# Windowed attention and gated network over 192 tiles: softmax in the score banks, small value products on two row groups, network input in its own bank, new orders

## The reference

```
for i in range(6):
    x = attn_layer(shift_tokens(x), Wqkv[i], q_scale[i], k_scale[i], Wo[i]) + x
    x = ffn_layer(shift_tokens(x), ln_g[i], ln_b[i], W1[i], b1[i], W2[i], b2[i]) + x

attn_layer:
    q, k, v = split(x @ Wqkv)                  # 16 heads of 64
    q = l2norm(q) * q_scale;  k = l2norm(k) * k_scale
    q, k = rotary(q), rotary(k)                # q*cos*scale + rotate_half(q)*sin*scale
    sim  = q @ k of the own and the previous window of 32 rows, masked
    out  = softmax(sim) @ v;   return out @ Wo
ffn_layer:
    xn = (x - mean) / sqrt(var + 1e-5) * g + b
    a, gate = split(xn @ W1 + b1);  return a * gelu(gate) @ W2 + b2
```

## Time and profile before

| what | value |
|---|---|
| median of 3 runs (lowest to highest) | 3764.9 us (3754.34 to 3772.09) |
| the profiled execution | 3773.0 us |
| its span, first to last instruction | 3771.0 us |
| mean granted TensorE clock | 0.962 |
| busy: PE, DVE, ACT, POOL | 3375.2, 3287.8, 2435.9, 2810.7 us |

### The profile page before, as it was taken

How to read it: one execution, slowest core, us unless ns; L and a number is a source line. 1 busy time by engine, 2 the same in 40 slices (tenths; PEclk the granted TensorE clock), 3 DMA queues, 4 the chain that set the end, 5 groups by cost and what they waited for, 6 DMA issues and landing times.

```text
span 3771.0 us, 107872 instructions
## 1 busy us (share of the span) xinstructions
PE 3375.2 (90%) x45916; PEld 2204.0 (58%) x46108; DVE 3287.8 (87%) x2914; ACT 2435.9 (65%) x3945; POOL 2810.7 (75%) x1265
## 2 busy tenths in 40 slices
PE   5758999998999999999998999899999999999987
PEld 3325665665665665665666666565666656666664
DVE  6758999998999988999898998898988988998992
ACT  4645766766766766666666676666666666666764
POOL 4457788778787778778777778877777887887771
PEclk9879999999999999999999999999999999999996
DMA  2001111121111111111111111121111111111111
GB/s 72 1 1 36 36 34 38 34 58 41 35 34 39 34 51 44 39 34 35 36 52 44 33 35 35 31 50 44 39 33 34 38 46 45 39 37 35 34 37 36
DMA packets 129694, 141.98 MB, mean 38 GB/s; under 512 B 35388, under 2 KB 73152, under 8 KB 129216
## 3 DMA queue, kind: packets, MB, share of 16 engines
q1 hardware_dynamic: 129216, 135.09, 14.5%
HBM read 19.62 MB, written 2.10 MB: 6 GB/s over the span
## 4 chain that ended last, share of the span: by engine, by line
PE 33%; DVE 23%; POOL 18%; issue 12%; ACT 4%; SPq 3%; DMA 2%; POOLq 0%; ACTq 0%; DVEq 0%
PE bank L570 10%; POOL rr L1138 8%; POOL swp L1148 5%; PE mid L620 4%; DVE Pr L1362 4%; DVE rot L1398 4%; PE mid L579 4%; DVE raw L1390 4%; PE bank L639 4%; PE bank L668 3%; DVE rot L1404 3%; PE mid L607 2%; PE mid L627 2%; DVE ss L1384 2%; PE bank L676 2%
## 5 line engine op out<-in xcount | busy, mean ns | idle before, releaser
L1148 POOL TENSOR_TENSOR swp<-raw,TS 128x1024 f32<-128x1024 f32 x384 | 899.6, 2370 | 622.0 <-DVE raw L1390 622.0
L570 PE MATMUL bank<-wqkv,xs 128*128 128x512 f32 x2304 | 1206.9, 627 | 24.1 <-DMA xs<-F 8.6
L1138 POOL TENSOR_TENSOR rr<-ssm,nhalf 128x32 f32<-128x32 f32 x192 | 1214.8, 6327 | 16.0
L896 ACT ACTIVATE raw<-bank 128x512 f32<-128x512 f32 x768 | 434.6, 592 | 545.0 <-DVE rot L1404 483.8
L579 PEld LDWEIGHTS mid<-ident,rot 128*128 128x128 f32 x3072 | 367.8, 143 | 387.7 <-issue 335.9
L579 PE MATMUL mid<-ident,rot 128*128 128x128 f32 x3072 | 444.6, 278 | 132.7 <-DVE rot L1404 127.3
L1384 DVE TENSOR_REDUCE ss<-sq 128x16 f32<-128x1024 f32 x384 | 463.6, 1207 | 112.1 <-ACT sq L904 111.3
L570 PEld LDWEIGHTS bank<-wqkv,xs 128*128 128x128 f32 x2304 | 387.3, 193 | 289.9 <-issue 194.0
L1390 DVE TENSOR_TENSOR raw<-raw,rr 128x2048 f32<-128x2048 f32 x192 | 469.3, 2444 | 42.6 <-POOL rr L1138 42.6
L1398 DVE TENSOR_TENSOR rot<-raw,TC 128x2048 f32<-128x2048 f32 x192 | 442.2, 2303 | 52.6 <-PE mid L579 51.1
L1404 DVE TENSOR_TENSOR rot<-rot,swp 128x2048 f32<-128x2048 f32 x192 | 440.2, 2292 | 21.0 <-DVE rot L1398 1.4
(11 more groups left out here) (132 smaller groups left out, 4340.8 us busy)
## 6 DMA issues: line engine op xcount, KB each, us to landing
PT<-PTd SPq DMA_DIRECT2D x1344, 64.0 KB
xs<-F SPq DMA_DIRECT2D x192, 64.0 KB, 1.9
BT<-PTd SPq DMA_DIRECT2D x192, 64.0 KB
wqkv<-d_wqkv SPq DMA_DIRECT2D x36, 256.0 KB, 2.8
fwo<-d_fwo SPq DMA_DIRECT2D x6, 512.0 KB, 4.3
d_out<-X SPq DMA_DIRECT2D x8, 256.0 KB, 2.3
w<-d_w SPq DMA_DIRECT2D x6, 341.0 KB
w<-d_w SPq DMA_DIRECT2D x6, 128.0 KB
```

The costliest lines, as they stand in the source:

```text
L570: nc.tensor.matmul(bank[bk][:, :], xs[:, j, :], wqkv[:, c, :], start=True, stop=True)\
L1138: pool.tensor_tensor(rr[:, :], ssm[:, :], nhalf[:, :], ALU.pow).then_inc(rr_ready, 1)
L1148: last = pool.tensor_tensor(dst[:, :, :, t, :], src[:, :, :, 1 - t, :], tab.unsqueeze(2).broadcast_to([P, 2, HEADS, 32]), ALU.mult)
```

## The change

1. `less_max` writes its result back into banks 3 and 4 instead of `Pr`; `exps`, `sums` and the input of `probs` are in the banks too. PE's `scores` of the next tile therefore waits for `probs` (`prob_ready`) and no longer for `less_max` (`sub_ready`).
2. `BT` is filled in two parts (heads of u < 4 on partitions 96 to 127, of u >= 4 on partitions 64 to 95), and a new tile `VT` holds the previous tile's last V rows for u >= 4 on partitions 64 to 95. The small products alternate between the two row groups and between banks 2 and 5. A tile of j > 0 has 10 DMAs instead of 8, one of j = 0 has 7.
3. `centred` is written to bank 7, which the network's other products use, instead of bank 6; `out_proj` of a batch's first tile waits for `attn_to_sbuf` and no longer for `ffn_normed`.
4. New orders on all engines. `qk_back` 2 and 3 move one slot earlier. ACT's first copy of a tile waits for `cos_part` and `sin_part` of the tile two before and no longer for `rotated`.

More of the change, by code:

```diff
@@ L417, in loads_and_moves @@
                 next_ffn(l)
-                for q in range(5):
+                for q in range(6):
                     for i in range(TPB):
@@ L439, in _ @@
                 fetch(DEPTH, m)
-            for m in range(-5, 0):
+            for m in range(-4, 0):
                 move(DEPTH, m)
@@ L693, in slot @@
                     step(c, 2, qk_back, 0, True)
[L694 to L697, removed]
+                    after(c, (3, qkT_out[1]), (5, oT_out), (3, qkT_out[3]))
+                    step(c, 2, qk_back, 3, False)
+                    after(c, (0, raw_out[0]), (4, v_out[0]), (1, raw_out[3]))
@@ L698, in slot @@
+                    step(c, 0, proj, 3, False, 1)
+                    after_batch(c, (3, yo_ready), (3, lin_out[2]), (3, ge_ready[2]), (3, ge_ready[1]), (3, ge_ready[0]), (3, lin_out[0]), (3, lin_out[1]), (3, nT_out), (3, xn_ready))
+                    batch(c, 2, centred)
                     after(c, (2, qkT_out[0]), (3, qkT_out[2]), (5, oT_out))
-                    after(c, (3, qkT_out[3]), (3, qkT_out[1]), (5, oT_out))
+                    after(c, (2, qkT_out[3]), (3, qkT_out[1]), (5, oT_out))
@@ L722, in slot @@
-                    batch(c, 2, ffn_in, 0, 1, False, 7)
-                    after(c, (4, sub_ready))
-                    step(c, 3, scores)
+                    after(c, (4, prob_ready))
+                    step(c, 3, scores)
+                    after(c, (4, v_out[0]), (1, raw_out[3]), (1, raw_out[0]))
+                    step(c, 0, proj, 0, False, 1)
+                    after_batch(c, (2, xn_ready), (3, yo_ready), (3, lin_out[2]), (3, ge_ready[2]), (3, ge_ready[1]), (3, ge_ready[0]), (3, lin_out[0]), (3, lin_out[1]), (3, nT_out))
@@ L804, in slot @@
+                    step(c, 2, qk_back, 2, False)
                     step(c, 4, out_proj)
@@ L1006, in slot @@
                     step(c, 4, o_to_sbuf)
                     step(c, 0, squares, 1)
+                    step(c, 3, to_v, 4)
+                    step(c, 2, qk_to_sbuf, 2)
+                    step(c, 3, to_v, 5)
                     step(c, 2, qk_to_sbuf, 1)
-                    step(c, 3, to_v, 4)
+                    batch(c, 2, ffn_normed)
                     batch(c, 2, ffn_affine)
-                    step(c, 3, to_v, 5)
-                    step(c, 2, qk_to_sbuf, 2)
-                    step(c, 2, qk_to_sbuf, 3)
@@ new lines, in slot @@
+                    step(c, 3, exps)
+                    batch(c, 2, lin_to_sbuf, 0)
+                    step(c, 0, to_raw, 3, False)
+                    step(c, 4, o_to_sbuf)
+                    step(c, 0, squares, 1)
+                    step(c, 3, to_v, 4)
+                    step(c, 2, qk_to_sbuf, 2)
+                    batch(c, 2, gelu, 0)
+                    batch(c, 2, gelu, 1)
+                    step(c, 3, to_v, 5)
+                    batch(c, 2, gelu, 2)
+                    step(c, 2, qk_to_sbuf, 1)
+                elif c % TPB == 2:
+                    step(c, 0, to_raw, 1, True)
@@ L1424, in slot @@
                     step(c, 3, sums)
+                    batch(c, 2, ffn_stats)
                     step(c, 3, sums_inverse)
+                    step(c, 3, probs)
                     step(c, 0, sumsq, 1)
-                    step(c, 3, probs)
                     step(c, 3, probs_back)
@@ L1466, in slot @@
                     step(c, 1, rotated)
-                    batch(c, 1, ffn_stats)
                     step(c, 2, maxes)
@@ L1470, in slot @@
                     step(c, 0, normed)
-            slots(4, slot)
+            slots(8, slot)
             for b in range(B - 2, B):
```

269 lines of the change are left out of this document (124 added, 145 removed).

## The result

| what | value |
|---|---|
| median of the changed kernel's runs (lowest to highest) | 3612.2 us (3608.0 to 3612.9) |
| median of the kernel before, same chip | 3761.3 us (3754.3 to 3772.1) |
| ratio, with its 95% interval | 0.961 (0.958 to 0.964) |
| the profiled execution, its span | 3608.0 us, 3606.2 us |
| mean granted TensorE clock | 0.980 |

The change makes the kernel 149 us faster, 4%. The forecast was 3645 us, range 3500 to 3775.

What follows compares the result with a forecast made beforehand. DVE and PE, filled nearly alike, were taken as the bound. DVE work 62.8, gaps 1.0 and waits 5.4 make 69.2 us per batch against 71.7; 2.5 x 48 = 120 off 3765 gives 3645 us, range 3500 to 3775.

Steps and rivals of the forecast that it cites:

- Part 1: Softmax in the banks: `probs` falls from 1.88 to 1.22 us, `less_max` and `exps` stay at 1.22 and 1.05.
- the doubling rival: In-place bank operations cost double: DVE gets 4.9 us more per batch, 74.1, or 3880 us; chance 0.03.
- The new wait for `probs`: PE's `scores` waits for `probs`: nothing in slots 1 to 3, at worst 1 us per batch in slot 0.
- 2.4 per batch on DVE (65.2 becomes 62.8): DVE's busy time per batch in us, with some 0.6 us off `probs` in each of 4 tiles.
- the sum: DVE's batch: work 62.8, gaps 1.0, waits 5.4, together 69.2 us against 71.7 before.
- Part 2: Small products on two row groups: 0.55 us instead of 1.05, 1.5 us off PE per batch.
- fits below: PE's work of 64.6 us per batch stays under DVE's 69.2.
- the 1 to 2 named: `pv` on PE stands 1 to 2 us for band DMAs in slots 1 and 3.
- Part 3: Network in bank 7 and `rstd` early: the stall of `ffn_normed` for `rstd` goes, 1.9 us off the mean batch.
- long batch: A batch of 75.4 us where an ordinary one takes 70.0, with `ffn_normed` waiting 3.9 us for `rstd`.
- Part 4: New waits of the order, from ACT's copies and gelus in slots 1 and 2: 5.4 us of DVE waits per batch.
- The slower rival: ACT's chain in slots 1 and 2 stalls PE 4.5 us and lowers the clock every batch: 3851 us; chance 0.12.

Runs made afterwards that it cites:

- a_no_small: The changed kernel with the small products back on one row group and 8 band DMAs per tile: 3620.9 us, ratio 0.965.
- b_wait: The kernel before with one wait more, DVE's `normed` waits for `rstd` in slot 3: 3770.4 us, ratio 1.003.
- the orders alone: The changed kernel with softmax back in SBUF and small products on one row group, keeping new orders and the network's bank: 3743.7 us, ratio 0.999.
- a_act: The changed kernel with two swaps on ACT, `to_v` 5 ahead of gelu 1 and `qk_to_sbuf` 1 ahead of gelu 2: 3491.3 us, ratio 0.931.
- part 1 alone in the old order, b_banks: The kernel before with only the softmax in the banks, orders and small products as before: 3870.3 us, ratio 1.032.

## Why the prediction was right

The direction, the size (3645 against 3612) and the named mechanisms held. Step by step:

**Part 1.** `probs` at 1.22 with no spread, `less_max` in place 1.232, `exps` in the banks 1.02 in the mean: the in-place price was right, the doubling rival fell. The new wait for `probs` cost next to nothing (weight loads for `scores` wait 7.2 us for it from 600 to 3400 us, never over 0.2). But "2.4 per batch on DVE (65.2 becomes 62.8)" was short: DVE is busy for 61.7. `normed` lost 0.17 x 4 and `cos_part` 0.04 x 4 too, 0.8 of the missing 1.1 us, which I had not counted, though the earlier trace rows showed `normed` and `vpe` in collision. 1.1 us x 48 = 53 us is the mis-sized term of the sum; the waits, 0.4 us longer than walked, take back 19 of it.

**Part 2.** 0.60 us measured for the 0.55 taken; 32 products at 18.8 ns. The saving in PE is 1.35 us per batch. The forecast let products at 1.05 cost 0.8 us per batch (38 us); a_no_small lost 9 to 15, so that bound was too wide, but a_no_small takes the two DMAs back as well. PE's work "fits below" held. `pv` waits for its DMAs 0.9 us in the mean in slot 1 (40 times in 42 batches, 1.7 at most), at the lower end of the 1 to 2 named, and in slot 3 only 9 times, 0.6 us each: there the forecast had one wait too many. The Trainium skill's floor in "TensorE: Matmul & The Clock Gate", section "Wait — 56ns, not 53.3ns?" (about 25 ns between starts) would give 0.80, an estimate from the page's figure; this trace does not agree, with 18.8 ns.

**Part 3.** No long batch is left. That `rstd` early is worth 1.9 us per mean batch cannot be read off alone: b_wait takes the long batches away in another manner and gains nothing, and the orders alone gain nothing either. So the 1.9 is there only when nothing else takes its place, which the sum took for granted.

**Part 4.** `maxes` waits 3.87 us once per batch (walked: 3.7), PE stands 1.26 and 1.04 us (walked: 1.4 and 0.8). All waits of DVE from 600 to 3500 us are 246 us (`maxes` 187.8, `sums` 31.9, `sumsq` 26.5) in 42.4 batches, 5.8 each for the 5.4 forecast. They are not all the ones walked: `maxes` 4.4 for 3.7 + 0.8, `sumsq` 0.6 for 0.9, and 0.8 at `sums`, which the walk had at nothing. 61.7 + 1.0 + 5.8 = 68.5, the mean batch from 600 to 3400 us (68.2 over all 47). a_act showed that the chain causes 2.3 of the 3.87; what is left of it, 1.5, stays.

**Where it was right by luck.** The prediction gives each part a price per batch. The experiments show that this is not how this kernel answers: part 1 alone in the old order costs 123 us. The sum came out because I walked DVE's batch in the new order (work, gaps, waits), which takes the whole, and not because the parts had these prices singly. Two errors also ran against each other, 1.1 us too much DVE work and 0.4 too few waits. The slower rival had its place right (gelu 1 ahead of `to_v` 5, gelu 2 ahead of `qk_to_sbuf` 1) and its point of decision wrong: PE's stands stayed at 2.3 us and the clock at 1.00.

## What to carry to other kernels

Where two engines are released by the same event and one blocks the other, a faster engine can win the race in each round instead of in some, and whatever waits for the loser pays: look for such a pair before taking work off an engine, and price parts of a change only together with the order in which they will stand. An operation that collides is not mended by moving it until every neighbour is looked at; here, taking its input out of the shared memory mended it. And once a hand walk has named a chain across engines, turn it around at once: two pairs of steps exchanged on ACT and one DMA issued earlier were worth as much (158 us, 151 by the ratios) as the whole change (149 us).

## What the runs showed of the hardware

- DVE reading and writing the same PSUM banks in one `tensor_tensor` of 128x1024 takes 1.232 us, against 1.224 when it writes to SBUF, and ACT's exponential in place 1.01 to 1.02 us in the mean against 1.05 in SBUF.
- POOL's power (`rr`, 5.46 us) is blocked by DVE only in its start: 7.48 when it starts behind a `rotated`, else 5.46 with `cos_part` and `rotated` running beside it.
- 32 products of 32 rows, alternating between two row groups and two banks, take 0.60 us, 18.8 ns each; in order on one row group 1.05 us, 33 ns each. Whether the row groups or the banks bring it was not separated.
- A DVE operation with two SBUF inputs (`probs`) that starts within POOL's `sin_part` stands until that ends and then takes its 1.1 to 1.2 us: 2.8 in the mean for 1.2.
- In the kernel before and in b_banks the granted clock fell to its lower level (1.2 GHz), mostly where PE had just stood 3.6 to 4.5 us, for 3.4 or 6.8 us each time, and `out_proj` then took up to 3.2 us for 1.95. In the changed kernel, with PE's stands of 1.0 to 1.7 us, it stayed at 1.00 from 600 to 3400 us.
